# Five engine lists and the table of PSUM banks of an attention pipeline, replaced by others

## Chip, core and metric

One core of a Trainium2 chip runs one program. The metric is the device time of an execution in microseconds (us); the time before is the median of three runs.

## What is computed

For 64 sequences of 128 tokens with 256 features, three transformer layers of 8 heads (32 wide) run first, then one cross attention of 16 heads (16 wide). Layer 0 takes its queries, keys and values from `ctx`, layer 1 from `x`; layer 2 takes queries and keys from layer 1's result and values from layer 0's. Layers 0 and 2 have a feed-forward part of 1024 hidden features. The attention of a layer makes two softmaxes, with a decay by distance between them:

```python
sc = softmax(where(damb, scores, NEG)) * masks
distcum, disttot = cumsum(sc, -1), sum(sc, -1, keepdims=True)
dist = sqrt(clip((disttot - distcum) * pos, 0, None))
te = clip(exp(dist * gamma), 1e-05, 100000.0)
scores = softmax(where(masks, scores * te, NEG))
x = layernorm(query + (scores @ v) @ oW.T + ob)
if apply_pos:
    x = layernorm(x + relu(x @ w1.T + b1) @ w2.T + b2)
```

## The kernel before, in words

All weights stay in SBUF. Two sequences make a group, and 32 groups go through one software pipeline. A group's work is cut into steps, and each engine has a list of steps that it goes through once per turn: `TENSOR` (line 43), `SCALAR` (58), `VECTOR` (75), `POOL` (93, GpSimd) and `SYNC` (99, the DMA queue). An entry is a delay and a step: in turn `it` the step is done for group `it - delay`, so a turn works on up to three groups. `run_turns` (257) writes out the first three turns and the last two; the turns between them are the body of a hardware loop of each engine. Between the end of its list and its start, therefore, an engine takes the loop's branch. Lists are cyclic: only the place of a step among the others, its group, and the place of the branch matter.

The steps, with the unit in brackets, (layer, sequence) or (3, sequence, half) for the cross attention:

- TensorE: `scores` (the product of queries and keys, into one of two large PSUM tiles), `pt` (four of the eight head tiles of the probabilities are transposed; halves 0 and 1), `att` (probabilities times values, and the transposed reciprocals), `o`, `k`, `v`, `kx`, `vx`, `q` (projections), `turn` (a normalized result is transposed: `turn l 1` behind the attention of layer l, `turn l 2` behind its feed-forward part), `up` (a quarter of the hidden features each) and `down`.
- VectorE: `max1`, `dist` (a scan of 1024 columns, line 920), `x` (eight products, line 929), `scores2` (939), `max2` (945), `recip` (951), `sums` (residual, statistics and scaling, lines 964 to 977) and `tok` (991) of a norm.
- ScalarE: `exp1`, `exp2` (eight exponentials with sums, line 802), `ln`, `root`, `effect` (821, 826, 831), `spread` (842).
- GpSimd: `select` (the mask, 1052), `widen` (the reciprocals widened for `att`, 1066 and 1069), `dev` (1076, 1078).
- What TensorE writes to a small PSUM bank is copied out (`pt`, `k`, `v`, `kx`, `vx`, `q`, `turn`, `up`, at lines 450 to 489) by the engine in whose list the step stands, ScalarE or VectorE; `att` is read by VectorE after `spread`, `o` and `down` by its `sums`.

A layer's unit goes scores, max1, exp1, dist, x, ln, root, effect, scores2, select, max2, exp2, pt, recip, widen, att. `sums l 1` needs `o l`, `dev` needs `sums`, `tok` needs `dev`, and `turn` needs `tok`.

Fifty-eight of TensorE's 68 steps use the four small banks; `BANKS` (104) names the bank of each in the order of `TENSOR`. A step waits until the bank's previous content has been read:

```python
i = GEN_BANK[step]
pe.wait_ge(gen_free[i], gen_order[i].before(now, d, step))
```

`att` also waits for its `widen`, for the copies of both `pt` halves and of its values (`attend`); `up` waits for the copy of `turn` (`in_sbuf`). `down` reads the hidden quarters 0, 1, 2, 3 in this order and waits for each. Every engine works strictly in the order of its list, so that a step that waits holds all behind it. `check_reuse` (219) tests the order for buffers that have no wait of their own.

In `TENSOR` before, the steps around the waits that matter stand so, with bank and copying engine: down 2 [2], att(0,1) [2], att(0,0) [1], turn 2 2 [0, VectorE], o 0 [3], pt(1,0) 0; and vx [0, ScalarE], pt(3,0,1) 0, turn 1 1, pt(3,0,1) 1, pt(3,0,0) 0 [0].

Of the kernel before, what the change touches and what calls it, by code (L numbers as in the profile page):

```python
# [74 lines left out]
VECTOR = [(1, ("max2", (2, 0))), (1, ("sums", 0, 2)), (1, ("scores2", (2, 1))), (0, ("max1", (0, 0))),  # L75
    (1, ("recip", (2, 0))), (1, ("tok", 0, 2)), (2, ("att", (3, 1, 1))), (2, ("att", (3, 0, 0))),
    (1, ("max2", (2, 1))), (0, ("max1", (0, 1))), (0, ("dist", (0, 0))), (0, ("k", 1)), (1, ("kx",)),
    (0, ("x", (0, 0))), (1, ("v", 2)), (2, ("att", (3, 1, 0))), (0, ("dist", (0, 1))), (1, ("recip", (2, 1))),
# [3 lines left out]
    (0, ("dist", (1, 0))), (0, ("x", (1, 0))), (0, ("dist", (1, 1))), (0, ("recip", (0, 1))), (0, ("x", (1, 1))),  # L82
    (0, ("scores2", (1, 0))), (1, ("sums", 2, 2)), (0, ("max2", (1, 0))), (0, ("scores2", (1, 1))),
    (1, ("tok", 2, 2)), (0, ("att", (0, 0))), (0, ("att", (0, 1))), (0, ("max2", (1, 1))), (1, ("turn", 2, 2)),
    (2, ("tok", 3, 1)), (0, ("recip", (1, 0))), (0, ("sums", 0, 1)), (0, ("pt", (1, 0), 1)), (0, ("recip", (1, 1))),
    (0, ("pt", (1, 1), 0)), (1, ("max1", (3, 0, 1))), (0, ("tok", 0, 1)), (0, ("att", (1, 0))), (0, ("att", (1, 1))),
# [6 lines left out]
POOL = [(1, ("widen", (2, 0))), (1, ("widen", (2, 1))), (0, ("select", (0, 0))), (1, ("dev", 2, 1)),
    (0, ("select", (0, 1))), (0, ("widen", (0, 0))), (0, ("widen", (0, 1))), (0, ("select", (1, 0))),
    (1, ("dev", 2, 2)), (0, ("select", (1, 1))), (2, ("dev", 3, 1)), (0, ("widen", (1, 0))), (0, ("widen", (1, 1))),
    (0, ("dev", 0, 1)), (0, ("dev", 1, 1)), (1, ("widen", (3, 0, 1))), (0, ("select", (2, 0))),
    (1, ("widen", (3, 0, 0))), (1, ("widen", (3, 1, 0))), (1, ("widen", (3, 1, 1))), (0, ("dev", 0, 2)),
    (0, ("select", (2, 1)))]
SYNC = [(1, ("load", "pad_mask")), (0, ("load", "ctx_f")), (2, ("diag", (3, 1, 0))), (2, ("diag", (3, 1, 1))),
    (1, ("diag", (2, 0))), (1, ("diag", (2, 1))), (1, ("load", "cx_f")), (0, ("load", "ctx_t")),  # L100
    (0, ("diag", (0, 0))), (0, ("diag", (0, 1))), (0, ("load", "x_f")), (1, ("load", "pad_bias")),
    (0, ("diag", (1, 0))), (0, ("diag", (1, 1))), (1, ("diag", (3, 0, 0))), (1, ("diag", (3, 0, 1))),
    (0, ("load", "x_t")), (2, ("store",))]
BANKS = [3, 0, 2, 1, 0, 1, 2, 3, 2, 1, 2, 3, 1, 0, 3, 2, 3, 1, 0, 2, 3, 2, 0, 1, 3, 2, 3, 2, 0, 1, 3, 0, 2, 2, 1, 0,
    3, 2, 1, 0, 3, 1, 2, 3, 2, 1, 0, 3, 1, 2, 0, 1, 0, 3, 1, 2, 0, 2]
# [1017 lines left out]
```

## Time and profile before

| | us |
|---|---|
| median of 3 runs | 3373.02 (3371.89 to 3376.1) |
| the profiled execution | 3372.7 |
| its span | 3371.0 |
| TensorE busy | 2990.0, 89% |
| VectorE busy | 2802.8, 83% |
| ScalarE busy | 2715.9, 81% |
| GpSimd busy | 775.8, 23% |
| mean granted TensorE clock | 0.97 |

The profile is of one execution. Busy time counts an instruction from its start to its end, and ends overlap the next start a little. Idle time ahead of an instruction is put down to what released it. The granted clock is the share of TensorE's full clock that was given in a stretch.

### The profile page before, as it was taken

What the parts mean: (1) busy time and instruction counts of PE and PEld (TensorE: products, weight loads), DVE (VectorE), ACT (ScalarE), POOL (GpSimd) and SP (SyncE); (2) the same over time, 40 slices, a digit from 0 to 9 for tenths busy, and PEclk for the clock granted to TensorE, in tenths of its full rate; (3) what the DMA queues carried; (4) which work ended last, traced back from release to release, by engine and by line L of the source; (5) the groups of instructions that cost most, each with busy time, mean ns of one, the idle gap of its engine ahead of it and who ended that gap; (6) DMA issues with size and microseconds to landing.
All of it is one profiled execution on the core that took longest, in us unless ns stands there. A gap on an engine that the chain in (4) does not pass through costs nothing.

```text
span 3371.0 us, 71476 instructions
## 1 busy us (share of the span) xinstructions
PE 2990.0 (89%) x19520; PEld 2204.6 (65%) x19520; DVE 2802.8 (83%) x5825; ACT 2715.9 (81%) x10244; POOL 775.8 (23%) x1111
## 2 busy tenths in 40 slices
...
DMA packets 166407, 101.66 MB, mean 30 GB/s; under 512 B 36697, under 2 KB 165709, under 8 KB 166221
## 3 DMA queue, kind: packets, MB, share of 16 engines
...
q14 instruction: 167, 1.36, 0.1%
...
## 4 chain that ended last, share of the span: by engine, by line
PE 55%; DVE 19%; issue 12%; SPq 4%; ACT 3%; DMA 2%; POOL 1%; DVEq 0%; ACTq 0%; POOLq 0%
PE gen_ps L623 17%; PE gen_ps L755 13%; PE gen_ps L709 6%; PE gen_ps L673 4%; SPq L556 4%; PE gen_ps L690 3%; DVE E L920 3%; PE scores_ps L664 2%; ACT X L802 2%; PE scores_ps L652 2%; DVE X L929 2%; PE gen_ps L718 2%; PE gen_ps L631 2%; PE gen_ps L684 2%; DVE res L964 2%
## 5 line engine op out<-in xcount | busy, mean ns | idle before, releaser
L802 ACT ACTIVATE X<-X,nm 128x128 f32<-128x128 f32 x1536 | 596.0, 405 | 56.7 <-DVE nm L945 55.8
L802 ACT ACTIVATE E<-scores_ps,nm 128x128 f32<-128x128 f32 x1536 | 542.3, 406 | 24.2 <-DVE nm L912 24.0
L912 DVE TENSOR_REDUCE nm<-scores_ps 128x8 f32<-128x1024 f32 x320 | 390.3, 1220 | 182.0 <-PE scores_ps L652 113.6
L623 PE MATMUL gen_ps<-f_buf,up_w 128*128 128x256 f32 x2048 | 466.1, 383 | 0.8 <-ACT f_buf L459 0.8
L1052 POOL TENSOR_SCALAR_AFFINE_SELECT X<-X 128x1024 f32<-128x1024 f32 x192 | 211.2, 1100 | 1100.8 <-DVE X L939 1100.0
L755 PE MATMUL gen_ps<-down_w,hidden 128*128 128x256 f32 x2048 | 459.7, 379 | 0.0
L802 ACT ACTIVATE X<-scores_ps,nm 128x128 f32<-128x128 f32 x1024 | 362.3, 400 | 116.6 <-issue 60.9
L673 PE MATMUL gen_ps<-ident,X 128*128 128x128 f32 x2560 | 380.0, 283 | 79.2 <-ACT xv_t L476 39.8
L929 DVE SCALAR_TENSOR_TENSOR X<-E,rz,decay 128x128 f32<-128x128 f32 x1536 | 431.0, 350 | 3.7 <-DVE E L920 0.5
L920 DVE TENSOR_TENSOR_SCAN E<-chain,E 128x1024 f32<-128x1024 bf16 x192 | 429.8, 2238 | 0.0
L623 PEld LDWEIGHTS gen_ps<-f_buf,up_w 128*128 128x128 f32 x2048 | 382.7, 191 | 70.5 <-issue 21.9
L673 PEld LDWEIGHTS gen_ps<-ident,X 128*128 128x128 f32 x2560 | 293.5, 143 | 201.9 <-issue 104.8
L755 PEld LDWEIGHTS gen_ps<-down_w,hidden 128*128 128x128 f32 x2048 | 381.7, 190 | 55.5
L450 ACT COPY probs_f<-gen_ps 128x512 f32<-128x512 f32 x448 | 257.2, 610 | 150.6 <-PE gen_ps L673 148.0
L802 ACT ACTIVATION_READ_ACCUMULATOR E<-scores_ps,nm 128x1 f32 x1536 | 377.7, 246 | 0.0
L1066 POOL TENSOR_SCALAR rz_wide<-rz 128x128 f32<-128x128 f32 x256 | 191.3, 763 | 573.3 <-DVE rz L951 573.3
L802 ACT ACTIVATION_READ_ACCUMULATOR X<-X,nm 128x1 f32 x1536 | 312.3, 203 | 0.0
L945 DVE TENSOR_REDUCE nm<-X 128x8 f32<-128x1024 f32 x192 | 232.3, 1210 | 59.5 <-POOL X L1052 59.5
L802 ACT ACTIVATION_READ_ACCUMULATOR X<-scores_ps,nm 128x1 f32 x1024 | 246.0, 240 | 0.0
L709 PE MATMUL gen_ps<-o_w,att_f 128*128 128x256 f32 x768 | 238.0, 444 | 5.6 <-DVE att_f L455 5.5
L821 ACT ACTIVATE X<-X,root_floor 128x1024 f32<-128x1024 f32 x192 | 232.1, 1209 | 13.0 <-DVE X L929 13.0
L652 PE MATMUL scores_ps<-k_diag,k_f 64*128 64x256 f32 x1536 | 221.8, 408 | 14.6 <-DMA k_diag<-k_f 12.7
...
## 6 DMA issues: line engine op xcount, KB each, us to landing
...
xk_diag<-xk_f SPq DMA_DIRECT2D x1024, 8.0 KB, 1.8
...
```

The lines of the kernel that those rows point to most:

```text
L450: last = copy(probs_f[:, P_SLOT[u], half * BANK:(half + 1) * BANK], ps[:, :])
L623: mm = nc.tensor.matmul(ps[:, i * T:(i + 1) * T], w[:, k, c * P:(c + 1) * P], src[:, k, :], start=(k == 0), stop=(k == C - 1))
L652: mm = nc.tensor.matmul(out[:, bank * BANK + c * 2 * S:bank * BANK + (c + 1) * 2 * S], k_f[l % 2][rows, c, b * S:(b + 1) * S], k_diag[rows ...
L673: mm = nc.tensor.transpose(ps[:, j * S:(j + 1) * S], X[:, X_SLOT[u], i * S:(i + 1) * S], ident[:, :])
L709: nc.tensor.matmul(out, att[:, b, c, :], w[:, c, :], start=(c == 0), stop=False)
L755: nc.tensor.matmul(out, hidden[:, f, b * S:(b + 1) * S], down_w[l][:, f, :], start=(f == 0), stop=False)
L802: a = nc.scalar.activation(dst[:, cols], src[:, cols], ACT.Exp, bias=minus_max[:, h:h + 1], accum_out=sums[:, h:h + 1])
L821: nc.scalar.activation(x, x, ACT.Ln, bias=root_floor[:, :]).then_inc(ln_done, 1)
L912: nc.vector.tensor_reduce(nm1[:, UNIT[u], :], unit_heads(scores_ps[SLOT[u]][:, :]), AX_X, ALU.max, negate=True).then_inc(max1_done, 1)
L920: nc.vector.tensor_tensor_scan(e, chain[FIRST_KEY_MASK[u[0]]][:, ::-1], e, 0.0, ALU.mult, ALU.add).then_inc(scan_done, 1)
L929: ins = nc.vector.scalar_tensor_tensor(out=X[:, p, i * S:(i + 1) * S], in0=E[:, E_SLOT[u], i * S + 1:(i + 1) * S + 1], scalar=rz1[:, UNIT[ ...
L945: nc.vector.tensor_reduce(nm2[:, UNIT[u], :], unit_heads(X[:, X_SLOT[u], :]), AX_X, ALU.max, negate=True).then_inc(max2_done, 1)
```

## The change

The five lists and the bank table are replaced; nothing else is. All steps are the same and so is their number on TensorE, GpSimd and the DMA queue. Twelve copies change engine: `pt(0,1)` 0 and 1, `turn 2 1`, `v 0`, `vx` and `pt(2,0)` 1 go from ScalarE to VectorE; `turn 2 2`, `pt(1,0)` 1, `pt(1,1)` 0, `v 1`, `v 2` and `up 2 0` go from VectorE to ScalarE (six each way). The loop's branch of each list stands at another place. The diff, cut to the parts that are spoken of:

```diff
-TENSOR = [(1, ("up", 0, 2)), (1, ("up", 0, 3)), (0, ("k", 0)), (1, ("down", 0)), (2, ("att", (3, 0, 0))),
-    (0, ("scores", (0, 0))), (2, ("pt", (3, 1, 0), 0)), (2, ("pt", (3, 1, 0), 1)), (2, ("att", (3, 1, 1))),
...
-    (1, ("up", 2, 0)), (1, ("up", 2, 2)), (1, ("up", 2, 1)), (1, ("up", 2, 3)), (0, ("pt", (0, 1), 0)),
-    (0, ("pt", (0, 1), 1)), (1, ("down", 2)), (0, ("att", (0, 1))), (0, ("att", (0, 0))), (1, ("turn", 2, 2)),
-    (0, ("o", 0)), (0, ("pt", (1, 0), 0)), (1, ("q",)), (0, ("pt", (1, 0), 1)), (0, ("pt", (1, 1), 0)),
...
-SCALAR = [(2, ("exp1", (3, 0, 0))), (2, ("vx",)), (1, ("turn", 1, 1)), (2, ("pt", (3, 0, 1), 0)),
...
-    (1, ("exp1", (3, 0, 1))), (0, ("turn", 0, 1))]
...
+    (2, ("pt", (3, 1, 1), 0)), (0, ("k", 0)), (1, ("up", 0, 1)), (1, ("up", 0, 2)), (2, ("att", (3, 0, 0))),
+    (2, ("pt", (3, 1, 1), 1)), (1, ("down", 0)), (0, ("scores", (0, 0))), (2, ("pt", (3, 1, 0), 0)),
+    (2, ("pt", (3, 1, 0), 1)), (2, ("att", (3, 1, 1))), (0, ("k", 1)), (0, ("scores", (0, 1))), (1, ("turn", 0, 2)),
+    (1, ("pt", (2, 0), 0)), (1, ("kx",)), (1, ("pt", (2, 0), 1)), (2, ("att", (3, 1, 0))), (1, ("v", 2)),
+    (1, ("pt", (2, 1), 0)), (0, ("v", 1)), (1, ("pt", (2, 1), 1)), (0, ("v", 0)), (1, ("att", (2, 0))),
+    (1, ("att", (2, 1))), (0, ("scores", (1, 0))), (1, ("o", 2)), (0, ("scores", (1, 1))), (0, ("pt", (0, 0), 0)),
+    (0, ("pt", (0, 0), 1)), (2, ("o", 3)), (1, ("turn", 2, 1)), (1, ("up", 2, 0)), (1, ("up", 2, 1)),
+    (1, ("up", 2, 2)), (1, ("up", 2, 3)), (0, ("pt", (0, 1), 0)), (0, ("pt", (0, 1), 1)), (1, ("down", 2)),
+    (0, ("att", (0, 1))), (0, ("att", (0, 0))), (0, ("pt", (1, 0), 0)), (0, ("pt", (1, 0), 1)), (1, ("turn", 2, 2)),
...
+SCALAR = [(1, ("ln", (1, 0))), (2, ("up", 2, 3)), (1, ("root", (1, 0))), (1, ("effect", (1, 0))),
+    (1, ("ln", (1, 1))), (1, ("root", (1, 1))), (1, ("effect", (1, 1))), (1, ("exp2", (1, 0))),
...
+    (0, ("exp2", (0, 1))), (1, ("up", 2, 1)), (1, ("up", 2, 0)), (1, ("up", 2, 2))]
+VECTOR = [(2, ("recip", (3, 0, 1))), (2, ("max1", (3, 1, 1))), (2, ("pt", (3, 0, 0), 1)), (1, ("max1", (2, 0))),
...
+    (1, ("scores2", (2, 0))), (2, ("recip", (3, 1, 1))), (2, ("att", (3, 0, 0))), (2, ("pt", (3, 1, 1), 1)),
+    (1, ("max2", (2, 0))), (1, ("sums", 0, 2)), (0, ("max1", (0, 0))), (1, ("scores2", (2, 1))), (1, ("tok", 0, 2)),
+    (0, ("k", 1)), (1, ("max2", (2, 1))), (0, ("max1", (0, 1))), (0, ("dist", (0, 0))), (2, ("att", (3, 1, 1))),
+    (1, ("pt", (2, 0), 1)), (1, ("kx",)), (0, ("x", (0, 0))), (0, ("dist", (0, 1))), (1, ("recip", (2, 1))),
+    (2, ("att", (3, 1, 0))), (1, ("recip", (2, 0))), (0, ("x", (0, 1))), (0, ("scores2", (0, 0))), (0, ("v", 0)),
+    (1, ("att", (2, 0))), (1, ("att", (2, 1))), (0, ("max2", (0, 0))), (0, ("max1", (1, 0))),
+    (0, ("scores2", (0, 1))), (1, ("sums", 2, 1)), (0, ("max1", (1, 1))), (1, ("tok", 2, 1)), (0, ("max2", (0, 1))),
+    (1, ("turn", 2, 1)), (0, ("dist", (1, 0))), (2, ("sums", 3, 1)), (0, ("x", (1, 0))), (0, ("dist", (1, 1))),
+    (0, ("x", (1, 1))), (0, ("scores2", (1, 0))), (0, ("pt", (0, 1), 0)), (0, ("recip", (0, 0))),
+    (0, ("pt", (0, 1), 1)), (0, ("max2", (1, 0))), (0, ("recip", (0, 1))), (1, ("sums", 2, 2)),
+    (0, ("scores2", (1, 1))), (1, ("tok", 2, 2)), (0, ("att", (0, 1))), (0, ("att", (0, 0))), (0, ("max2", (1, 1))),
...
+    (1, ("pt", (3, 0, 1), 1)), (1, ("vx",)), (1, ("pt", (3, 0, 0), 0))]
+POOL = [(2, ("widen", (3, 1, 1))), (2, ("widen", (3, 1, 0))), (1, ("dev", 0, 2)), (1, ("select", (2, 1))),
+    (1, ("widen", (2, 1))), (1, ("widen", (2, 0))), (0, ("select", (0, 0))), (1, ("dev", 2, 1)),
+    (0, ("select", (0, 1))), (2, ("dev", 3, 1)), (0, ("select", (1, 0))), (0, ("widen", (0, 0))),
+    (0, ("widen", (0, 1))), (1, ("dev", 2, 2)), (0, ("select", (1, 1))), (0, ("widen", (1, 0))), (0, ("dev", 0, 1)),
...
```

In the new table of banks, down 2 has bank 0, att(0,1) bank 1 and att(0,0) bank 0; v 2 and v 0 have bank 0; up 2 0 to up 2 3 have banks 3, 0, 2 and 1.

## Rows read from the trace of the kernel before

**Rows 1.** The page: busy time of each engine.
```profile
PE 2990.0 (89%) x19520; PEld 2204.6 (65%) x19520; DVE 2802.8 (83%) x5825; ACT 2715.9 (81%) x10244; POOL 775.8 (23%) x1111
```

**Rows 2.** Busy time in both parts of one turn (start:end, length, engines).
```profile
1514.20:1566.70 52.50, 47.34 (x303) 34.19 (x304) 40.35 (x83) 39.69 (x158) 10.19 (x18) 0.97 0.11 33
1566.70:1614.70 48.00, 44.88 (x310) 34.04 (x308) 46.66 (x100) 44.99 (x163) 13.80 (x17) 1.00 0.08 22
sum 100.50, PE 92.22 PEld 68.23 DVE 87.00 ACT 84.69 POOL 23.98; mean PE 46.11 PEld 34.12 DVE 43.50 ACT 42.34 POOL 11.99
```

**Rows 3.** TensorE's waits over the run: total us, times, longest.
```profile
PE gen_ps L718 <- DVE x_tok L991: 115.0, 34, 4.3
...
PE gen_ps L673 <- ACT xv_t L476: 39.8, 28, 1.9
```

**Rows 4.** TensorE in order of time, one turn: start, length, instructions, [idle].
```profile
1514.19 0.43 PE L684 MATMUL gen_ps<-ident,rz_wide 128*128 128x128 f32 x2 [1.11 <-DVE res L964]
...
1519.56 1.11 PE L718 MATMUL gen_ps<-ident,x_tok 128*128 128x128 f32 x4 [3.42 <-DVE x_tok L991]
1520.47 1.91 PE L709 MATMUL gen_ps<-o_w,att_f 128*128 128x256 f32 x4
...
1532.15 1.13 PE L709 MATMUL gen_ps<-o_w,att_f 128*128 128x256 f32 x4
...
1534.20 0.60 PE L718 MATMUL gen_ps<-ident,a_tok 128*128 128x128 f32 x4
...
1541.11 0.66 PE L673 MATMUL gen_ps<-ident,X 128*128 128x128 f32 x4 [1.45 <-ACT xv_t L476]
...
1566.71 0.27 PE L684 MATMUL gen_ps<-ident,rz_wide 128*128 128x128 f32 x1
...
1581.71 0.66 PE L673 MATMUL gen_ps<-ident,X 128*128 128x128 f32 x4 [0.67 <-DVE v_t L469]
...
1585.85 0.44 PE L684 MATMUL gen_ps<-ident,rz_wide 128*128 128x128 f32 x2 [0.43 <-POOL rz_wide L1066]
```

**Rows 5.** Stretches around the longest wait, with TensorE's granted clock.
```profile
1519.50:1523.50 4.00, 3.94 (x15) 3.20 (x16) 3.30 (x8) 2.65 (x15) 1.26 (x4) 0.61 0.00 0
...
1530.60:1541.00 10.40, 9.07 (x50) 5.65 (x46) 6.91 (x15) 7.13 (x37) 1.69 (x3) 1.00 0.05 13
```

**Rows 6.** VectorE in order of time, same turn.
```profile
1513.12 0.76 DVE L964 TENSOR_TENSOR res<-gen_ps,a_tok 128x256 f32<-128x256 f32 x2
...
1521.22 0.68 DVE L459 COPY h_buf<-gen_ps 128x512 f32<-128x512 f32 x1
...
1565.70 1.22 DVE L945 TENSOR_REDUCE nm<-X 128x8 f32<-128x1024 f32 x1 [1.36 <-POOL X L1052]
1566.91 0.76 DVE L964 TENSOR_TENSOR res<-gen_ps,a_tok 128x256 f32<-128x256 f32 x2
...
1580.98 0.68 DVE L469 COPY v_t<-gen_ps 128x512 f32<-128x512 f32 x1
...
1602.07 0.87 DVE L487 TENSOR_SCALAR hidden<-gen_ps,up_bias 128x256 f32<-128x256 f32 x2
```

**Rows 7.** VectorE's kinds with their shapes, 1566.8 to 1614.7 us.
```profile
L991 DVE SCALAR_TENSOR_TENSOR a_tok<-res,rstd,norm_b 128x256 f32<-128x256 f32 x2 | 1.7, 892 | 0.0
...
L991 DVE SCALAR_TENSOR_TENSOR y_tok<-res,rstd,norm_b 128x256 f32<-128x256 f32 x2 | 0.8, 453 | 0.0
```

**Rows 8.** ScalarE in order of time, at its loop's end.
```profile
1534.84 0.58 ACT L459 COPY f_buf<-gen_ps 128x512 f32<-128x512 f32 x1 [0.97 <-PE gen_ps L718]
1537.62 0.37 ACT L802 ACTIVATE X<-scores_ps,nm 128x128 f32<-128x128 f32 x1 [2.20 <-issue]
```

**Rows 9.** Waits of all engines over the run, longest first.
```profile
ACT X L802 <- issue: 60.9, 28, 2.6
```

**Rows 10.** GpSimd in order of time, same turn.
```profile
1509.87 1.09 POOL L1066 TENSOR_SCALAR rz_wide<-rz 128x128 f32<-128x128 f32 x2 [4.25 <-DVE rz L951]
...
1594.86 1.12 POOL L1052 TENSOR_SCALAR_AFFINE_SELECT X<-X 128x1024 f32<-128x1024 f32 x1 [0.78 <-DVE X L939]
```

More of the change, by code:

```diff
@@ L41 @@
 SEED = 1
-TENSOR = [(1, ("up", 0, 2)), (1, ("up", 0, 3)), (0, ("k", 0)), (1, ("down", 0)), (2, ("att", (3, 0, 0))),
[6 rows of a table removed]
-    (0, ("pt", (0, 1), 1)), (1, ("down", 2)), (0, ("att", (0, 1))), (0, ("att", (0, 0))), (1, ("turn", 2, 2)),
-    (0, ("o", 0)), (0, ("pt", (1, 0), 0)), (1, ("q",)), (0, ("pt", (1, 0), 1)), (0, ("pt", (1, 1), 0)),
-    (1, ("scores", (3, 0, 1))), (0, ("pt", (1, 1), 1)), (0, ("att", (1, 0))), (0, ("att", (1, 1))),
-    (1, ("scores", (3, 0, 0))), (0, ("o", 1)), (0, ("turn", 0, 1)), (1, ("scores", (3, 1, 0))), (1, ("vx",)),
[4 rows of a table removed]
@@ L58 @@
-SCALAR = [(2, ("exp1", (3, 0, 0))), (2, ("vx",)), (1, ("turn", 1, 1)), (2, ("pt", (3, 0, 1), 0)),
[7 rows of a table removed]
-    (1, ("pt", (2, 1), 1)), (0, ("root", (0, 0))), (1, ("spread", (2, 0))), (0, ("effect", (0, 0))),
-    (1, ("spread", (2, 1))), (0, ("ln", (0, 1))), (0, ("root", (0, 1))), (0, ("effect", (0, 1))),
[7 rows of a table removed]
[L75 to L78, printed above, removed]
[3 rows of a table removed]
[L82 to L86, printed above, removed]
[4 rows of a table removed]
-    (1, ("recip", (3, 1, 0))), (0, ("dist", (2, 0))), (0, ("x", (2, 0))), (0, ("dist", (2, 1))),
-    (1, ("recip", (3, 1, 1))), (0, ("x", (2, 1))), (0, ("scores2", (2, 0)))]
@@ L93 @@
[L93 to L105, printed above, removed]
+TENSOR = [(2, ("pt", (3, 0, 1), 0)), (2, ("scores", (3, 1, 0))), (1, ("turn", 1, 1)), (2, ("pt", (3, 0, 1), 1)),
+    (2, ("pt", (3, 0, 0), 0)), (1, ("k", 2)), (2, ("scores", (3, 1, 1))), (2, ("pt", (3, 0, 0), 1)),
+    (1, ("up", 0, 3)), (2, ("att", (3, 0, 1))), (1, ("scores", (2, 0))), (1, ("up", 0, 0)), (1, ("scores", (2, 1))),
+    (2, ("pt", (3, 1, 1), 0)), (0, ("k", 0)), (1, ("up", 0, 1)), (1, ("up", 0, 2)), (2, ("att", (3, 0, 0))),
[7 more added lines that the diff above has]
+    (0, ("att", (0, 1))), (0, ("att", (0, 0))), (0, ("pt", (1, 0), 0)), (0, ("pt", (1, 0), 1)), (1, ("turn", 2, 2)),
+    (0, ("o", 0)), (1, ("q",)), (0, ("att", (1, 0))), (0, ("pt", (1, 1), 0)), (0, ("pt", (1, 1), 1)),
+    (1, ("scores", (3, 0, 1))), (0, ("att", (1, 1))), (1, ("scores", (3, 0, 0))), (0, ("o", 1)), (0, ("turn", 0, 1)),
+    (1, ("vx",))]
```

15 lines of the change are left out of this document (added), and 41 rows, old and new, of tables (SCALAR, TENSOR, VECTOR).

## The prediction

> **What bounds the kernel now.** The page first: TensorE is busy 2990 us of 3371 [rows 1], the most loaded engine, but its idle time, 381 us, is what a new order could at best win. Then one turn of the loop, 100.5 us, cut where TensorE passes from one dense stretch to the next [rows 2]. From the start of att(0,1) to the end of down 0 (part 2, 52.5 us) TensorE is busy 47.3 us and VectorE only 40.4. From the end of down 0 to the next att(0,1) (part 1, 48.0 us) VectorE is busy 46.7. So neither engine bounds the turn alone: VectorE paces part 1, TensorE with its waits paces part 2.
>
> The waits of the whole run [rows 3] show the largest, 115 us for the normalized result of layer 2 (turn 2 2) and its like, and 40 us for ScalarE's copy of vx. The turn in order of time [rows 4] gives each its size: 1.11 us ahead of att(0,1), which sits in down 2's bank and so waits for VectorE's sums 2 2; 3.42 ahead of turn 2 2; 1.45 for the copy of vx; 0.67 and 0.43 for the copy of v 2 and for widen; 0.84 ahead of turn 2 1 is of the same kind and stands in no row shown. Together about 8 us. One more loss hides in busy time: behind the 3.42 us wait the granted clock is 0.61 for 4.0 us, elsewhere 1.00 [rows 5], and turn 2 2 and o 0 take 1.11 and 1.91 us for what takes 0.60 and 1.13 later [rows 4]. That is 4.0 x 0.39 = 1.5 us a turn. The waits of 1.11 and 1.45 us have no such drop.
>
> **The change, part 2 of the turn.** I count against 52.5 us.
> - turn 2 2 now has both halves of pt(1,0) ahead of it, and VectorE does no max2 between sums 2 2 and tok 2 2. From the start of sums 2 2 to the end of tok 2 2 it does 2.4 us of sums, scores2 1.2, and tok 1.7. TensorE does att(0,1), att(0,0) and the two pt halves meanwhile, about 3 us. I leave 1.3 us of the wait, o 0 included: -3.4 + 1.3 = -2.1.
> - With a wait of 1.3 us, near the 1.11 and 1.45 that cost no clock, the clock stays up: -1.5.
> - vx is copied by VectorE and pt(3,0,1) 1 no longer shares its bank; pt(3,0,0) 1, the next user, comes behind k 2 and a scores step: -1.4.
> - att(3,0,0) moves here from part 1: +0.8 (1566.71 to the scores behind it).
> - ScalarE's branch leaves this part, VectorE's comes in, between pt(3,0,0) 0 and max1(3,1,1). The trace shows ScalarE idle 2.20 us at its branch with nothing to wait for [rows 8], 60.9 us in 28 turns [rows 9]. For VectorE nothing is to be seen: ahead of max2(2,0), the first step of its list, it waits for a mask anyway (1565.70). So the price on VectorE is between 0 and 2.2. I take 1.5, of which the slack around k 2 covers all but 0.4 at scores(2,1), whose PSUM tile exp1(3,1,1) frees: +0.4. The cover is thin: if it goes, exp1(3,1,1), then exp1(2,0) and layer 2's whole chain up to sums 0 2 are late.
>
> Part 2: 52.5 - 2.1 - 1.5 - 1.4 + 0.8 + 0.4 = 48.7 us.
>
> The Trainium skill (Runtime: NRT & Kernel Launch, Instruction fetch mechanics) says that a taken branch whose target is outside the two pages at hand stalls until the target is fetched. The trace agrees for ScalarE, 2.2 us; by that rule VectorE's branch would show it as well.
>
> **The change, part 1 of the turn.** sums 0 2 starts at 1566.91 and the next sums 2 2 at 1513.12 + 100.5 = 1613.6, 46.9 us behind the end of down 0 [rows 6], at most 1.3 of them idle [rows 2].
> - VectorE's work between these two changes: out go att(3,0,0) 0.3, v 1 and v 2 0.68 each, up 2 0 0.87; in come pt(2,0) 1, v 0, turn 2 1 and both halves of pt(0,1), 0.68 each, and max2(1,0), 1.22, that came behind sums 2 2 [rows 6] (the copies of 512 columns are those at 1521.22 and 1580.98). Sum: +4.6 - 2.5 = +2.1.
> - tok 0 2 now comes right behind scores2(2,1), whose mask GpSimd is then writing. A tok beside such a mask took 892 ns an instruction, another 453 [rows 7]: +0.8.
> - Idle time squeezed out: -1.3.
> - ScalarE's branch now stands between up 2 2 and ln(1,0), and up 2 3 behind that. TensorE reaches the ups later than before, for widen(2,0) comes behind widen(2,1), 1.1 us each [rows 10], and the ups wait for turn 2 1's copy, behind max2(0,1) in VectorE's list with nothing on TensorE between. I place up 2 2's copy at 39.5 us, then 2.2 of branch, ln 1.2, up 2 3 0.8, root and effect 2.1: effect(1,0) at 45.8. VectorE is through with x(1,1) at about 44.5 and waits: +1.2.
>
> sums 2 2 would start at 46.9 + 2.1 + 0.8 - 1.3 + 1.2 = 49.7 us. att(0,1) no longer waits for it, since its bank differs, but for widen(0,1), whose recip stands right ahead of sums 2 2: 1.1 more, 50.8. TensorE alone would be there at about 45. So part 1 grows from 48.0 to 50.8; the shorter waits inside it (v 2, widen, turn 2 1, 1.11 at att(0,1)) win nothing, as VectorE's list is what lasts.
>
> **Sum.** 50.8 + 48.7 = 99.5 us a turn for 100.5. With 32 groups that is 32 x 1.0 = 32 us off 3372.7 (the profiled execution, which is the median 3373.0 to 0.3): **3340 us**. The fill and the drain keep their order but for small moves; I put them at nothing, within 10 us. The DMA queue keeps its distances (k 2's copy to the diag blocks of layer 2, 4 us), at nothing, covered by four steps of TensorE.
>
> **Rivals.**
> - *VectorE is not as late* (0.28). Were the branch hidden by ScalarE's backlog (0 instead of 1.2), and tok clear of the mask (0 instead of 0.8), part 1 would be 48.8 and the turn 97.5: 3277. Half of it gives 3309. For it: ScalarE is behind its work there, so its sequencer may run ahead. Against: the 2.2 us is there in each of 28 turns. I put it at 3295.
> - *VectorE's branch is exposed in full* (0.10): 2.2 instead of 1.5 delays scores(2,1) and then sums 0 2 by 0.7, 22 us: 3362. This is the skill's rule at full price.
> - *The clock drops at the new waits* (0.22), the case that ends slower. The order creates waits of some 2 us and more ahead of att(2,0) and att(0,1), between the 1.45 that cost no clock and the 3.42 that did [rows 4, 5]. A drop costs 1.5. Behind att(0,1) it lies on the path: 101.0, 3389. A second one behind att(2,0) passes partly to VectorE through scores(1,1): 102.0, 3420. It decides at a total of 1.0 us a turn. I put it at 3400.
> - *No difference* (0.08): part 1 loses what part 2 wins, 3366 to 3379. That the lists do the same under other names is excluded: six copies go each way and the bank of att(0,1) is another.
>
> **Numbers.** The forecast's own range is 3320 to 3362, chance 0.32; with the branch rival, larger gains, no difference and the slower case the chances are 0.32, 0.10, 0.28, 0.08 and 0.22. About 0.2% (7 us) is what a measurement can tell from no change. Faster 0.70, same 0.08, slower 0.22. The range takes in the larger gain nearly to its end and the slower case up to its first drop and a part of the second: 3280 to 3402.
>
> **What would show it.** In the changed profile: att(0,1) waits for GpSimd's rz_wide and not for VectorE's res; turn 2 2 waits under 1.5 us and the granted clock behind it is 1.0; no wait on xv_t; ScalarE's gap with no releaser stands ahead of ln(1,0) (line 821), VectorE's, if any, ahead of recip or max1; VectorE is busy in part 1 to over 95%. I am wrong if part 1 is not longer than 48 us, or if part 2 is still over 50 us.

## The result, and the profile after

The changed kernel takes **3407.09 us** (median of 4 runs, 3403.45 to 3415.54), the kernel before, run beside it, 3373.78 (3371.89 to 3376.10). The ratio is 1.0102, interval 1.0081 to 1.0122: slower by 33 us, where I had forecast 33 us less. The profiled execution took 3403.45 us. Its page, beside [rows 1]:

```profile
span 3401.7 us, 71760 instructions
PE 2986.5 (88%) x19520; PEld 2177.6 (64%) x19520; DVE 2791.1 (82%) x5825; ACT 2731.7 (80%) x10244; POOL 729.3 (21%) x1111
```

TensorE is as busy as before (2986.5 us for 2990.0); the added time is idle. Where it lies is told by the copy of kx, once in each of the 32 groups. Its rows (line 471 of VectorE, count, durations, first and last start), before:

```profile
L471 DVE TENSOR_TENSOR xk_f<-gen_ps,pad_mask x32: 673/679/692, 169.2 to 3291.5; 128x512 f32<-128x512 f32 x32
```

and after:

```profile
L471 DVE TENSOR_TENSOR xk_f<-gen_ps,pad_mask x32: 672/675/680, 173.4 to 3326.7; 128x512 f32<-128x512 f32 x32
```

The first copy comes 4.2 us later, the rest behind the last one is 4.5 us shorter (79.5, 75.0), and the 31 distances grow from 100.7 to 101.7 us. So fill and drain are even, as forecast, and the turn is what is longer.

Both parts of one turn, cut as in [rows 2] (start:end, length, busy of each engine, granted clock; the first row is part 2, the second part 1):

```profile
core 0: us, PE busy (x) PEld busy (x) DVE busy (x) ACT busy (x) POOL busy (x), PEclk, DMA share, GB/s
1535.50:1584.70 49.20, 46.93 (x321) 33.53 (x322) 37.98 (x81) 39.77 (x159) 9.85 (x16) 1.00 0.15 43
1584.70:1636.60 51.90, 44.60 (x293) 33.44 (x291) 48.74 (x101) 45.44 (x164) 12.74 (x18) 1.00 0.05 13
```

Part 2 took 49.2 us (forecast 48.7), part 1 took 51.9 (forecast 50.8), together 101.1, and that in a turn whose clock stayed at 1.00. Most turns are longer, because the clock falls in them; see below. TensorE's waits over the run, beside [rows 3]:

```profile
PE gen_ps L684 <- POOL rz_wide L1066: 125.7, 65, 7.8
PE gen_ps L623 <- DMA ctx_f<-in_ctxT: 101.6, 32, 57.0
PE gen_ps L623 <- DVE f_buf L459: 33.9, 32, 1.1
PE gen_ps L631 <- DVE xatt_f L455: 33.9, 30, 1.2
PE scores_ps L646 <- DVE X L939: 30.4, 34, 7.5
PE gen_ps L718 <- DVE x_tok L991: 19.9, 15, 4.3
PE gen_ps L755 <- ACT hidden L489: 12.5, 29, 0.6
```

The large wait of before is nearly gone (x_tok, 115.0 to 19.9), and the one for vx's copy is gone. In their place stand two: for `widen`, two in a turn, and one that the forecast did not have, for the transfer of ctx_f. Without its first time (57.0, the start of the kernel, the same before) that is 44.6 us in 31 turns. The same in order of time, beside [rows 4] (start, length, instructions, [idle before <- releaser]):

```profile
1504.43 0.44 PE L684 MATMUL gen_ps<-ident,rz_wide 128*128 128x128 f32 x2 [1.54 <-POOL rz_wide L1066]
...
1510.79 0.60 PE L646 MATMUL scores_ps<-dam_bias,ident_bf 128*128 128x512 bf16 x2 [0.66 <-DVE X L939]
...
1517.24 7.17 PE L623 MATMUL gen_ps<-f_buf,up_w 128*128 128x256 f32 x32 [1.07 <-DVE f_buf L459]
...
1528.33 1.13 PE L755 MATMUL gen_ps<-down_w,hidden 128*128 128x256 f32 x4 [0.45 <-ACT hidden L489]
...
1535.51 0.44 PE L684 MATMUL gen_ps<-ident,rz_wide 128*128 128x128 f32 x2 [2.38 <-POOL rz_wide L1066]
...
1539.43 0.66 PE L718 MATMUL gen_ps<-ident,x_tok 128*128 128x128 f32 x4 [0.92 <-DVE x_tok L991]
...
1570.99 1.99 PE L623 MATMUL gen_ps<-ctx_f,k_w 128*128 128x256 f32 x8 [1.25 <-DMA ctx_f<-in_ctxT]
```

The rows are att(2,0), scores(1,1), up 2 0, down 2 (its last hidden quarter, the copy of up 2 3), att(0,1), turn 2 2 and k 0. Why k 0 waits is seen in the DMA queue (the time is that of issue):

```profile
1560.67 5.91 SPq L556 DMA_DIRECT2D k_diag<-k_f  x8
1566.94 0.36 SPq L579 DMA_DIRECT2D pad_mask<-in_pad  x1
1567.64 0.38 SPq L572 DMA_DIRECT2D ctx_f<-in_ctxT  x1
```

The load stands behind the eight diag blocks of layer 2, which wait for k 2's copy. At 1567.64 it is issued, and 3.35 us later k 0 starts. In the kernel before, load and k 0 read:

```profile
1524.96 0.37 SPq L572 DMA_DIRECT2D ctx_f<-in_ctxT  x1
1557.79 1.96 PE L623 MATMUL gen_ps<-ctx_f,k_w 128*128 128x256 f32 x8
```

There the load had 32.8 us. Two edits of the change meet here. The order of the queue is another: `SYNC` before issued this load ahead of the diag blocks of (3,1,0), (3,1,1), (2,0) and (2,1), and the new one issues it behind all of them:

```diff
-SYNC = [(1, ("load", "pad_mask")), (0, ("load", "ctx_f")), (2, ("diag", (3, 1, 0))), (2, ("diag", (3, 1, 1))),
-    (1, ("diag", (2, 0))), (1, ("diag", (2, 1))), (1, ("load", "cx_f")), (0, ("load", "ctx_t")),
...
+SYNC = [(1, ("diag", (2, 1))), (1, ("load", "pad_mask")), (0, ("load", "ctx_f")), (0, ("load", "x_f")),
...
+    (1, ("diag", (3, 0, 0))), (1, ("diag", (3, 0, 1))), (1, ("diag", (3, 1, 0))), (1, ("diag", (3, 1, 1))),
+    (2, ("store",)), (0, ("diag", (2, 0)))]
```

And in the new `TENSOR` k 0 stands ahead of up 0 1 and up 0 2; before, it stood behind them.

**The clock.** From the busy time of TensorE between successive copies of kx, over the same 27 turns in the middle of each trace, and the granted clock of each such stretch (worked out from the view of windows; "full" is a turn whose mean granted clock is 1.00):

```
kernel                      turn us   PE busy   idle    full-clock turns
before                      100.91    92.66     8.25    0 of 27
after                       102.01    92.68     9.34    7 of 27
act_branch_moved            100.16    91.54     8.62    20 of 27
ctx_load_first              100.72    92.26     8.46    8 of 27
before_act_branch_moved      99.90    92.57     7.33    0 of 27
both_moved                   98.99    91.40     7.59    19 of 27
both_moved_widen_swapped     97.78    91.00     6.77    27 of 27
```

The busy time of a turn has not fallen. Before, the clock fell behind turn 2 2's wait of 3.42 us in each turn [rows 5]. After, it falls behind att(0,1)'s wait in 20 of the 27, behind att(2,0)'s in 4 and behind k 0's in 3; all of these are among the 20. One such turn, TensorE alone (start:end, length, busy, granted clock):

```profile
1395.00:1400.00 5.00, 3.46 (x30) 1.00 0.06 13
1400.00:1404.00 4.00, 4.00 (x42) 0.60 0.05 13
...
1428.00:1431.70 3.70, 1.39 (x7) 0.97 0.00 0
1431.70:1435.70 4.00, 3.94 (x42) 0.60 0.00 0
```

and its rows at both waits, att(2,0) and att(0,1):

```profile
1399.34 0.44 PE L684 MATMUL gen_ps<-ident,rz_wide 128*128 128x128 f32 x2 [1.54 <-POOL rz_wide L1066]
1399.71 0.64 PE L690 MATMUL gen_ps<-probs_f,v_t 128*32 128x128 f32 x16
1400.28 0.44 PE L684 MATMUL gen_ps<-ident,rz_wide 128*128 128x128 f32 x2
1400.65 1.02 PE L690 MATMUL gen_ps<-probs_f,v_t 128*32 128x128 f32 x16
...
1431.76 0.69 PE L684 MATMUL gen_ps<-ident,rz_wide 128*128 128x128 f32 x2 [2.38 <-POOL rz_wide L1066]
1432.38 1.08 PE L690 MATMUL gen_ps<-probs_f,v_t 128*32 128x128 f32 x16
...
1436.41 0.65 PE L718 MATMUL gen_ps<-ident,x_tok 128*128 128x128 f32 x4 [0.31 <-ACT probs_f L450]
```

The granted clock of 0.60 is a stretch mostly at 1.2 of TensorE's 2.4 GHz, and sixteen small products take 1.08 us for 0.64. The turn shown further up has waits of the same 1.54 and 2.38 us and no drop. There turn 2 2 starts 3.92 us behind the start of att(0,1), here (the last row) 4.65.

What a drop costs in time shows when the 27 turns are sorted by it (worked out from the view of windows and the timeline; cut at att(0,1) and at the end of down 0, means in us):

```
turns of the changed kernel           number   part 2   part 1
no drop                                  7     49.24    51.95
behind att(0,1) alone                   13     49.86    51.90
behind att(0,1) and att(2,0)             4     49.82    53.08
behind att(0,1) and k 0                  3     51.89    51.84
all                                     27     49.92    52.08
kernel before, all                      27     52.93    47.98
```

The wait for ctx_f is 1.2 to 1.4 us in some turns and 1.7 to 1.9 in others. Between turns of the same kind, a drop behind att(0,1) costs 0.5 us (49.67 for 49.17 with the short wait), one behind k 0 1.7 (51.89 for 50.19 with the long one), and one behind att(2,0) 1.2. Together that is (20 x 0.5 + 4 x 1.2 + 3 x 1.7) / 27 = 0.7 us a turn, some 23 us of the run. In the kernel before, a drop came in every turn and cost 1.5 (before_wait_filled). So the changed kernel loses less to the clock than the one before, and is slower all the same.

**ScalarE's branch.** It stands where the forecast put it, in two gaps with no releaser (ScalarE in order of time; up 2 2, ln(1,0) and up 2 3), beside [rows 8]:

```profile
1525.27 1.15 ACT L821 ACTIVATE X<-X,root_floor 128x1024 f32<-128x1024 f32 x1 [1.59 <-issue]
...
1527.44 0.84 ACT L489 ACTIVATE hidden<-gen_ps,up_bias 128x256 f32<-128x256 f32 x2 [1.02 <-issue]
```

Behind it comes effect(1,0), and VectorE waits for it ahead of scores2(1,0):

```profile
1530.34 1.22 DVE L939 SCALAR_TENSOR_TENSOR X<-X,scores_ps 128x1024 f32<-128x1024 f32 x1 [1.89 <-ACT X L831]
```

Over the run the waits read:

```profile
DVE X L939 <- ACT X L831: 63.6, 39, 2.4
ACT X L821 <- issue: 46.7, 28, 1.9
...
ACT hidden L489 <- issue: 26.2, 28, 1.1
```

So the branch takes 2.6 us a turn here ((46.7 + 26.2) / 28), where [rows 9] had 2.2.

### The profile page after: what moved, and what is told of

The parts are those of the page before. It is cut to its first block, busy times and chain, and to the rows that moved or that the text cites. A ratio compares the mean times of both kernels' runs of the same rounds, so it can differ in the third digit from the quotient of the medians.

```text
span 3401.7 us, 71760 instructions
## 1 busy us (share of the span) xinstructions
PE 2986.5 (88%) x19520; PEld 2177.6 (64%) x19520; DVE 2791.1 (82%) x5825; ACT 2731.7 (80%) x10244; POOL 729.3 (21%) x1111
## 4 chain that ended last, share of the span: by engine, by line
PE 27%; DVE 22%; issue 20%; ACT 14%; SPq 7%; POOL 5%; DMA 4%; DVEq 1%; POOLq 0%; ACTq 0%
PE gen_ps L623 9%; PE gen_ps L755 7%; SPq L556 5%; ACT X L802 4%; ACT E L802 4%; DMA ctx_f<-in_ctxT 3%; POOL rz_wide L1066 3%; DVE E L920 3%; DVE X L939 3%; PE gen_ps L673 2%; PE gen_ps L690 2%; DVE X L929 2%; DVE nm L912 2%; PE gen_ps L709 2%; ACT hidden L489 2%
## 5 line engine op out<-in xcount | busy, mean ns | idle before, releaser
L623 PE MATMUL gen_ps<-f_buf,up_w 128*128 128x256 f32 x2048 | 474.3, 385 | 33.9 <-DVE f_buf L459 33.9
L755 PE MATMUL gen_ps<-down_w,hidden 128*128 128x256 f32 x2048 | 467.5, 381 | 12.5 <-ACT hidden L489 12.5
L802 ACT ACTIVATION_READ_ACCUMULATOR X<-X,nm 128x1 f32 x1536 | 305.1, 199 | 0.0
L939 DVE SCALAR_TENSOR_TENSOR X<-X,scores_ps 128x1024 f32<-128x1024 f32 x192 | 232.9, 1213 | 64.0 <-ACT X L831 63.6
L450 ACT COPY probs_f<-gen_ps 128x512 f32<-128x512 f32 x416 | 235.0, 596 | 57.0 <-PE gen_ps L673 54.8
L821 ACT ACTIVATE X<-X,root_floor 128x1024 f32<-128x1024 f32 x192 | 220.2, 1147 | 70.0 <-issue 46.7
L1076 POOL TENSOR_TENSOR rstd<-moments,eps_col 128x2 f32<-128x2 f32 x192 | 65.0, 339 | 853.8 <-DVE moments L974 853.8
L489 ACT ACTIVATE hidden<-gen_ps,up_bias 128x256 f32<-128x256 f32 x448 | 183.3, 498 | 72.5 <-PE gen_ps L623 46.2
L684 PE MATMUL gen_ps<-ident,rz_wide 128*128 128x128 f32 x512 | 125.7, 309 | 125.7 <-POOL rz_wide L1066 125.7
```

The source lines that it names most:

```text
L450: last = copy(probs_f[:, P_SLOT[u], half * BANK:(half + 1) * BANK], ps[:, :])
L489: last = nc.scalar.activation(hidden[:, f, :], src, ACT.Relu, bias=bias)
L623: mm = nc.tensor.matmul(ps[:, i * T:(i + 1) * T], w[:, k, c * P:(c + 1) * P], src[:, k, :], start=(k == 0), stop=(k == C - 1))
L755: nc.tensor.matmul(out, hidden[:, f, b * S:(b + 1) * S], down_w[l][:, f, :], start=(f == 0), stop=False)
L802: a = nc.scalar.activation(dst[:, cols], src[:, cols], ACT.Exp, bias=minus_max[:, h:h + 1], accum_out=sums[:, h:h + 1])
L821: nc.scalar.activation(x, x, ACT.Ln, bias=root_floor[:, :]).then_inc(ln_done, 1)
```

## The experiments

**Theory** behind the first four runs: the loss has two sources that add, ScalarE's branch, now in layer 1's chain ln, root, effect, scores2, select, max2, exp2, and the late load of ctx_f. **Rivals:** part 1 is long because VectorE has more to do there, so that only its work counts; or the lost time is the clock's. An entry that goes from one end of its list to the other changes its delay by one, and the cyclic order stays; only the place of the branch moves. The median of the kernel before, run beside these, lies between 3373.28 and 3376.21 us; differences between kernels are good to some 3 us.

### act_branch_moved

```diff
-SCALAR = [(1, ("ln", (1, 0))), (2, ("up", 2, 3)), (1, ("root", (1, 0))), (1, ("effect", (1, 0))),
...
-    (0, ("exp2", (0, 1))), (1, ("up", 2, 1)), (1, ("up", 2, 0)), (1, ("up", 2, 2))]
+SCALAR = [(2, ("exp1", (3, 1, 1))), (1, ("up", 0, 3)), (2, ("spread", (3, 0, 1))), (1, ("exp1", (2, 0))),
...
+    (1, ("up", 2, 0)), (1, ("up", 2, 2)), (0, ("ln", (1, 0))), (1, ("up", 2, 3)), (0, ("root", (1, 0))),
...
+    (1, ("exp1", (3, 1, 0)))]
```

> The changed kernel with the start of ScalarE's list, and so its loop branch, moved to ahead of exp1(3,1,1), where ScalarE waits 3.2 us anyway; the cyclic order is the same. Theory (VectorE's list and the branch pace the stretch from down 0 to att(0,1)): the idle time of VectorE ahead of scores2(1,0), 1.89 us, and the wait of down 2 for up 2 3 go, the turn is 1.5 to 1.9 us shorter, some 3345 to 3360 us. Rival (the clock drops alone make it slow): TensorE's wait ahead of att(0,1) stays within 0.3 us and the time within 10 us of 3407.

Measured: 3354.59 us, ratio to before 0.9949 (0.9929 to 0.9968), 52 less than after. Both gaps with no releaser, ahead of ln(1,0) and of up 2 3, are gone, and VectorE's wait ahead of scores2(1,0) with them (`DVE X <- ACT X`, 63.6 to 13.9 us over the run). The forecast had put this branch at 1.2 us a turn on the path, 38 us. Of the 1.85 us that a turn wins in the table, 0.72 is idle time and 1.14 is busy time: 20 turns keep their clock, for 7. Ahead of att(0,1) TensorE now waits 1.12 us instead of 2.38, and no drop stands behind it.

### ctx_load_first

```diff
-SYNC = [(1, ("diag", (2, 1))), (1, ("load", "pad_mask")), (0, ("load", "ctx_f")), (0, ("load", "x_f")),
+SYNC = [(0, ("load", "ctx_f")), (1, ("diag", (2, 1))), (1, ("load", "pad_mask")), (0, ("load", "x_f")),
```

> The changed kernel with the load of ctx_f ahead of the four transfers of diag(2,1) in the DMA queue's list. Theory (k 0 waits for this load, 1.2 us a turn in the part that TensorE paces): k 0's wait goes, time 3407 minus 30 to 40 us, less what scores(2,1) then waits. Rival (VectorE is late for down 0's result as well, so that the wait is hidden): time within 10 us of 3407.

Measured: 3363.81 us, 0.9971 (0.9958 to 0.9983), 43 less than after. TensorE's waits:

```profile
PE gen_ps L621 <- DMA ctx_f<-in_ctxT: 56.8, 1, 56.8
...
PE scores_ps L650 <- DMA k_diag<-k_f: 24.6, 32, 4.3
```

The wait is left once, at the start. Part of it returns as a short wait for the diag blocks behind the load, (24.6 - 4.3) / 31 = 0.65 us a turn; the total is 43 us all the same. Part 2 takes 48.64 us in the mean for 49.92, and 48.32 for 49.24 in turns with no drop, so 0.9 us of the 1.3 a turn is won without the clock; the rest lies in turns with drops, where those behind k 0 are gone. Either edit alone makes the new order faster than before. That speaks against VectorE's added work as the cause: neither takes any of it away.

### before_act_branch_moved

The same in the kernel before: its `SCALAR` now starts at pt(1,1) 1.

```diff
-SCALAR = [(2, ("exp1", (3, 0, 0))), (2, ("vx",)), (1, ("turn", 1, 1)), (2, ("pt", (3, 0, 1), 0)),
+SCALAR = [(1, ("pt", (1, 1), 1)), (1, ("spread", (1, 0))), (1, ("spread", (1, 1))), (2, ("exp1", (3, 0, 1))),
+    (1, ("turn", 0, 1)), (2, ("exp1", (3, 0, 0))), (2, ("vx",)), (1, ("turn", 1, 1)), (2, ("pt", (3, 0, 1), 0)),
...
```

> The kernel before with only ScalarE's branch moved, to ahead of pt(1,1) 1, where ScalarE waits 2.35 us anyway. If the branch is what made vx late there, TensorE's wait of 1.45 us for xv_t goes and the time falls by 30 to 45 us to about 3335. Rival (the time goes into the next wait, for exp1 of the cross attention or for TensorE itself): within 10 us of 3374.

Measured: 3344.94 us, 0.9910 (0.9894 to 0.9927), 29 less. The wait for xv_t (39.8 us over the run [rows 3]) is gone; that of turn 2 2 stands (115.3), and no turn keeps its clock. So the branch costs 29 us at its old place and 52 at its new one, a net loss of 23 that the change made with it. Both kernels without an exposed branch are 10 us apart (3344.94, 3354.59).

### both_moved

Both edits in the new kernel.

> The changed kernel with both moves. If branch and load act in different parts of the turn, the gains add: 3310 to 3330 us. If one hides the other, the time is that of the better of the two.

Measured: 3318.60 us, 0.9834 (0.9818 to 0.9851), 88 less than after, where the single gains add to 96. They are two causes, nearly independent.

### both_moved_widen_swapped

The largest of TensorE's waits left in both_moved is `widen` (90.4 us over the run). The new lists do sequence 1 of layer 2 ahead of sequence 0 on VectorE and GpSimd, while att(2,0) comes first on TensorE.

```diff
 VECTOR
-(1, ("recip", (2, 1))), (2, ("att", (3, 1, 0))), (1, ("recip", (2, 0))),
+(1, ("recip", (2, 0))), (2, ("att", (3, 1, 0))), (1, ("recip", (2, 1))),
 POOL
-(1, ("widen", (2, 1))), (1, ("widen", (2, 0))),
+(1, ("widen", (2, 0))), (1, ("widen", (2, 1))),
```

> both_moved with recip and widen of (2,0) ahead of those of (2,1), the order in which att needs them. TensorE's wait of 1.54 us ahead of att(2,0) shrinks. If VectorE's list paces the stretch (theory), the time stays within 8 us of 3319; if TensorE's waits there count, it falls by 25 us or more.

Measured: 3282.96 us, 0.9728 (0.9712 to 0.9745), 36 less than both_moved and the fastest kernel of this study. My theory that the wait was covered by VectorE failed. In both_moved, att(2,0) starts late on TensorE (a turn at the full clock, as 19 of the 27 are):

```profile
1470.20 0.44 PE L683 MATMUL gen_ps<-ident,rz_wide 128*128 128x128 f32 x2 [1.54 <-POOL rz_wide L1065]
```

and behind it VectorE, which reads att(2,0) and att(2,1) at this place of its list, stands still too:

```profile
1471.75 0.42 DVE L454 TENSOR_TENSOR att_f<-gen_ps,att_f 128x256 f32<-128x256 f32 x1 [0.35 <-ACT att_f L841]
1472.69 0.42 DVE L454 TENSOR_TENSOR att_f<-gen_ps,att_f 128x256 f32<-128x256 f32 x1 [0.52 <-ACT att_f L841]
```

With `widen` in the order in which TensorE asks, TensorE waits 0.27 us and VectorE not at all:

```profile
1550.96 0.44 PE L683 MATMUL gen_ps<-ident,rz_wide 128*128 128x128 f32 x2 [0.27 <-POOL rz_wide L1065]
...
1553.37 0.85 DVE L454 TENSOR_TENSOR att_f<-gen_ps,att_f 128x256 f32<-128x256 f32 x2
```

In turns with no drop, part 1 takes 49.08 us for 49.95, and the difference is VectorE's 0.35 + 0.52. In the other 8 turns of both_moved the clock fell behind the wait of 1.54 us, and part 1 took 51.18; in the new kernel all 27 turns keep their clock. That is 8 x 1.23 / 27 = 0.4 us a turn more.

An engine whose list is the longest still loses what a late neighbour makes it wait, where it comes to the neighbour's result soon after.

### both_moved_dve_branch

both_moved with `VECTOR` rotated as well, to start at dist(2,1), a stretch in which VectorE has work without a pause.

```diff
-VECTOR = [(2, ("recip", (3, 0, 1))), (2, ("max1", (3, 1, 1))), (2, ("pt", (3, 0, 0), 1)), (1, ("max1", (2, 0))),
+VECTOR = [(1, ("dist", (2, 1))), (1, ("x", (2, 1))), (1, ("scores2", (2, 0))), (2, ("recip", (3, 1, 1))),
...
```

> both_moved with VectorE's branch moved from behind pt(3,0,0) 0 into a stretch where VectorE never waits, ahead of dist(2,1). In the changed kernel VectorE shows no gap at its branch. If its branch costs nothing (theory now), the time stays within 5 us of 3319 and there is no gap ahead of this dist. If it costs ScalarE's 2.2 us, which I had reckoned with at 1.5, and only slack hid it, the time rises by 40 to 60 us.

Measured: 3319.21 us, 0.9836 (0.9820 to 0.9853), 0.6 from both_moved. VectorE's branch costs nothing even there. At the place it has in the changed kernel no gap is seen either (VectorE in order of time, the last step of its list and the first):

```profile
1561.62 0.68 DVE L450 COPY probs_f<-gen_ps 128x512 f32<-128x512 f32 x1
1562.21 0.19 DVE L951 RECIPROCAL rz<-z 128x8 f32<-128x8 f32 x1
```

### after_wait_filled and before_wait_filled

What is the clock worth? TensorE gets dummy work while it waits: transposes of the identity into the bank that the step is about to write. They are added work and change nothing else. In the new kernel, ahead of att(0,1)'s waits:

```diff
+                if u == (0, 1):
+                    for _ in range(16):
+                        nc.tensor.transpose(ps[:, 0:S], ident[:, :], ident[:, :])
```

> The changed kernel with 16 transposes of the identity into att(0,1)'s own bank, ahead of its waits, which fill some 1.8 of the 2.4 us that TensorE stands still there; the result is overwritten. Theory (the clock falls behind this wait in most turns): the granted clock behind it is 1.0, mean busy time of the real work falls by about 1 us a turn, 3370 to 3390 us. Rival (the clock's drops there cost nothing, since VectorE paces what comes next): within 8 us of 3407.

Measured: 3407.86 us, 1.0101 (1.0084 to 1.0118), no gain. 18 of 27 turns now have the full clock, for 7, and the turn is as long as before the fill (102.03 us, 102.01). All 20 drops behind att(0,1) are gone, and in turns with no drop and the short wait for ctx_f part 2 takes 49.28 us, for 49.67 behind such a drop and 49.17 without one. So the fill wins 0.4 us where it prevents a drop and costs 0.1 where there was none. But the clock now falls behind k 0's wait in 5 turns for 3 and behind att(2,0)'s in 6 for 4, and the wait for ctx_f is long in 13 for 10; that takes the gain back (means of part 2 49.81 for 49.92, of part 1 52.22 for 52.08). In the kernel before, ahead of turn 2 2:

```diff
+                if (l, which) == (2, 2):
+                    for _ in range(24):
+                        nc.tensor.transpose(ps[:, 0:S], ident[:, :], ident[:, :])
```

> The kernel before with 24 such transposes ahead of turn 2 2's wait of 3.42 us, filling 2.8 of it. The price of the drop of the clock by itself, which I put at 1.5 us a turn: 3374 minus 35 to 50 us. Rival: less than 10 us, the slow stretch is covered by VectorE's chain.

Measured: 3324.84 us, 0.9853 (0.9837 to 0.9870), 49 less, 1.5 us a turn. The stretch that answers to the 0.61 of [rows 5] now reads:

```profile
1500.40:1504.40 4.00, 3.88 (x22) 1.00 0.00 0
```

The forecast's price of a drop, 1.5 us, is right where TensorE paces. Behind att(0,1) in the new kernel a drop costs a third of that: at the full clock turn 2 2 waits 0.92 us for VectorE's tok 2 2, and behind the drop at 1431.76 only 0.31, so that a part of what TensorE loses was idle time.

### after_widen_swapped

The changed kernel with the swap of `widen` and `recip` alone.

> The changed kernel with recip and widen of (2,0) ahead of those of (2,1), and nothing else. In both_moved the same edit gave 36 us. Theory (VectorE's list holds the reads of att(2,0) and att(2,1), so that a late widen is a wait of VectorE itself, in series with ScalarE's branch): the gain adds, 3365 to 3380 us. Rival (ScalarE, late by its branch, paces the stretch and hides it): over 3395.

Measured: 3385.12 us, 1.0030 (1.0019 to 1.0041), 22 less than after, between both expectations. In turns with no drop part 1 takes 51.11 us for 51.95, nearly the gain that it had in both_moved. What is missing is the clock: it now falls behind k 0's wait in 8 turns for 3, and part 2 takes 50.19 us in the mean for 49.92.

### best_att_early, best_att_and_turn_early

Can more be won from both_moved_widen_swapped? First att(3,1,1) earlier in `VECTOR`, since v 2 waits for its bank:

```diff
-(0, ("dist", (0, 0))), (2, ("att", (3, 1, 1))),
+(2, ("att", (3, 1, 1))), (0, ("dist", (0, 0))),
```

> both_moved_widen_swapped, and VectorE reads att(3,1,1) ahead of dist(0,0) instead of behind it. TensorE's wait of 1.13 us ahead of v 2, whose bank this frees, goes. If that wait is on the path: 3283 minus 20 to 35 us. If VectorE paces here (theory): within 8 us of 3283.

Measured: 3285.31 us, 0.9734 (0.9717 to 0.9750), no gain. TensorE's wait has the same length and another releaser, where both_moved_widen_swapped had `PE gen_ps L630 <- DVE xatt_f L454: 33.9, 30, 1.2`:

```profile
PE gen_ps L630 <- ACT v_t L468: 33.9, 31, 1.1
```

Then turn 2 1's copy ahead of max2(0,1) as well:

```diff
-(0, ("max2", (0, 1))), (1, ("turn", 2, 1)),
+(1, ("turn", 2, 1)), (0, ("max2", (0, 1))),
```

> best_att_early, and VectorE copies turn 2 1 ahead of max2(0,1) instead of behind it. TensorE's wait of 1.07 us ahead of up 2 0 shrinks by at most 0.4, since the turn is done only when max2 has begun; max2(0,1) and then exp2(0,1) come later by a wait of VectorE. Within 8 us of best_att_early, or up to 15 us slower.

Measured: 3309.02 us, 0.9806 (0.9790 to 0.9823), 24 slower than without it. The wait it was meant for shrank by 0.3 us (`DVE f_buf`, 34.1 to 25.4 us over the run), but those for `widen` grew, att(0,1)'s from 1.12 to 2.24 us:

```profile
PE gen_ps L683 <- POOL rz_wide L1065: 92.9, 94, 7.8
...
PE gen_ps L622 <- DVE f_buf L458: 25.4, 32, 0.9
```

from 59.4 us, and only 6 of 27 turns keep the full clock. A step moved ahead by one place was paid for elsewhere.

### before_branch_and_fill

The kernel before with its branch moved and its wait filled.

> The kernel before with ScalarE's branch ahead of pt(1,1) 1 and 24 transposes in turn 2 2's wait. One edit gave 29 us, the other 49. They act on different waits of TensorE, so they add: 3290 to 3305 us.

Measured: 3294.32 us, 0.9759 (0.9743 to 0.9775), 82 less than the kernel before beside it (3376.21), or 79 less than 3373.78; the single gains add to 78. So the old order reaches within 12 us of the best form of the new one.

## Why the prediction was wrong, point by point

The turn grew by 1.0 to 1.1 us where it was to shrink by 1.0.

- **"The DMA queue keeps its distances [...], at nothing, covered by four steps of TensorE."** This step failed, and its 43 us (ctx_load_first) is the largest loss that the forecast did not have at all. The queue did not keep its distances: `SYNC` was replaced with the other lists, and the load of ctx_f went from 32.8 us ahead of k 0 to 3.35, behind blocks that wait for k 2's copy. I had looked at what feeds the steps behind k 2, and neither at the load that the new `SYNC` moved nor at TensorE's own move of k 0, ahead of up 0 1 and up 0 2. This cause alone is more than the forecast's whole gain of 33.
- **ScalarE's branch, +1.2 in part 1.** Mis-sized. It took 2.6 us for 2.2, VectorE waited 1.89 for 1.2 in the turn shown, and its removal won 1.6 us a turn (52 us): 2.0 in part 1 (49.96 for 51.95 with no drop), of which part 2 gave 0.5 back (49.77 for 49.24), in part because turn 2 2 waits 1.24 us for 0.92. The branch at its old place, whose end is one of the gains in part 2, was worth 29 us.
- **Turn 2 2's wait, -2.1.** Right: 0.92 us is left in the turn shown, 1.3 was forecast.
- **"the clock stays up: -1.5."** Failed. The wait that dropped it is short, but att(0,1)'s, 2.38 us, drops it in 20 of 27 turns, and TensorE's busy time in a turn is what it was (92.66 and 92.68 us). This was the slower rival's mechanism, at its place. Its size, 1.5 at att(0,1) on the path, was wrong: a drop there costs 0.5. With those behind att(2,0) and k 0 the drops cost 0.7 us a turn on average, about half of the 1.5 that the forecast had taken as won.
- **vx, -1.4.** The wait is gone, as forecast.
- **VectorE's branch, +0.4, and the rival with 2.2.** Nothing: 0.6 us between two places. The Trainium skill (Runtime: NRT & Kernel Launch, Instruction fetch mechanics) has a taken branch outside the two pages at hand stall until the target is fetched; the traces agree for ScalarE, at 2.2 and 2.6 us, and show no stall for VectorE. Why the two differ, no run here tells.
- **tok beside the mask, +0.8.** Half right. The two instructions of tok 0 2 take 1.71 us together, for 0.83 before. But tok 2 1, which stood beside a mask before (892 ns an instruction in [rows 7], 1.70 us together), takes 1.25 now, so the net is 0.4:

```profile
1589.57 1.71 DVE L991 SCALAR_TENSOR_TENSOR y_tok<-res,rstd,norm_b 128x256 f32<-128x256 f32 x2
...
1615.30 1.25 DVE L991 SCALAR_TENSOR_TENSOR a_tok<-res,rstd,norm_b 128x256 f32<-128x256 f32 x2
```

- **widen(0,1), +1.1, and "the shorter waits inside it [...] win nothing, as VectorE's list is what lasts".** att(0,1) waits for `widen` as forecast. That waits inside part 1 are free is wrong: the one ahead of att(2,0), 1.54 us, which the new order made longer, costs 22 us in the changed kernel and 36 once the other two causes are gone.
- **The sums.** Part 2 at 49.2 for 48.7 looks nearly right by errors that cancel: 1.25 us of waiting for ctx_f that was not in it, against 0.4 for VectorE's branch that was not due and 0.4 that turn 2 2's wait is shorter than I left it. Part 1 is 51.9 for 50.8: VectorE waits 1.75 us for 1.2 at the branch, and 0.35 + 0.52 at the reads of att(2,0) and att(2,1), idle time that I had squeezed out; tok takes 0.4 less. The turns with drops add 0.7 us, which no part of the sum holds. Neither of the two signs of being wrong came (part 1 is 52.08 and part 2 49.92 in the mean): each looked at one part, and none at the whole turn.

The slower rival gave 3400 us, near the 3407 measured, and that is mostly luck. Its drops came where it had them and cost some 0.7 us a turn; but it set them on a turn of 99.5 us, and with no drop the turn is 101.2. The rest, and most of the loss, is a load, a branch and an order of two small steps. Taking these out one by one gives 3407, 3355 or 3364, 3319 and 3283 us.

**What stays open.** Why att(0,1)'s wait drops the clock in 20 turns and not in all, at the same length. What the new `SYNC` and the new place of k 0 each have in the late load: no run put back one without the other. VectorE's added work in part 1 was not tried by itself; with the three causes taken out, part 1 is 49.08 us, 1.1 above the kernel before.
